# Experts stage: ScalarE puts the tokens into the PSUM bank and writes the bank out; one gate product moves to GpSimd

## The reference

```python
x = x + conv_ref(ln_c(x))        # instance norm, q/k/v, attention in 8x8 windows (4 heads of 8), projection
t = tokens(x)                    # per pixel 32 channels
t = t + ffn_ref(ln_t(t))         # the mixture of experts
# ffn_ref: router_probs = softmax(t @ router_w + router_b)  over 8 experts
#   top_p, top_i = top_k(router_probs, 2); top_p /= sum(top_p)
#   out = sum_k top_p[k] * (t @ expert_w[top_i[k]] + expert_b[top_i[k]])
```

## Time and profile before

| what | value |
|---|---|
| median of 3 runs | 396.82 us (395.78 to 398.11) |
| profiled execution, its own time | 396.52 us |
| its span | 394.4 us |
| TensorE / VectorE / ScalarE / GpSimd busy | 90% / 85% / 66% / 41% of the span |

### The profile page before, as it was taken

How to read it: one execution, slowest core, us unless ns; L and a number is a source line. 1 busy time by engine, 2 the same in 40 slices (tenths; PEclk the granted TensorE clock), 3 DMA queues, 4 the chain that set the end, 5 groups by cost and what they waited for, 6 DMA issues and landing times.

```text
span 394.4 us, 12569 instructions
## 1 busy us (share of the span) xinstructions
PE 355.4 (90%) x5318; PEld 186.3 (47%) x5318; DVE 334.9 (85%) x435; ACT 260.4 (66%) x448; POOL 162.4 (41%) x191
## 2 busy tenths in 40 slices
PE   5998599999999999999999999898889897768894
PEld 2556366566666656566566556465321221111121
DVE  1598989898898889998998889999878999996785
ACT  3665787878878888768788887764663674324431
POOL 8610000220220220786551220687783468348543
PEclk9999999999999999999999999999998999896998
DMA  7700000220000000000002000033223444443541
GB/s 308 299 3 3 2 3 2 55 57 2 4 2 3 2 2 3 2 2 3 2 3 57 3 2 2 3 78 79 62 66 102 136 128 111 131 125 94 148 141 53
DMA packets 12870, 22.49 MB, mean 57 GB/s; under 512 B 2960, under 2 KB 5136, under 8 KB 12432
## 3 DMA queue, kind: packets, MB, share of 16 engines
q1 hardware_dynamic: 12240, 19.93, 17.4%
q10 hardware_dynamic: 576, 1.77, 1.1%
HBM read 5.96 MB, written 4.19 MB: 26 GB/s over the span
## 4 chain that ended last, share of the span: by engine, by line
PE 62%; DVE 23%; ACT 6%; issue 6%; POOL 2%; DMA 1%; POOLq 0%; DVEq 0%; ACTq 0%
PE psum L611 13%; PE psum L628 9%; PE psum L596 7%; PE psum L636 4%; PE psum L547 4%; PE psum L762 4%; PE psum L571 3%; DVE neg_max L1156 3%; PE psum L444 3%; DVE probs L1299 3%; PE psum L566 3%; DVE window_work L1159 3%; PE psum L580 2%; PE psum L774 2%; DVE probs L1296 2%
## 5 line engine op out<-in xcount | busy, mean ns | idle before, releaser
L327 POOL TENSOR_TENSOR o_norm<-o_tok,o_rden 128x128 f32<-128x128 f32 x64 | 25.4, 417 | 169.6 <-DVE o_rden L1169 169.6
L611 PE MATMUL psum<-weights_sb,window_work 128*128 128x128 f32 x512 | 81.6, 281 | 6.4 <-DVE window_work L1159 4.2
L896 ACT ACTIVATE probs<-psum 128x512 f32<-128x512 f32 x128 | 74.7, 594 | 17.5 <-PE psum L611 15.3
L1159 DVE TENSOR_TENSOR window_work<-psum,neg_max 128x1024 f32<-128x1024 f32 x64 | 78.4, 1225 | 2.2
L611 PEld LDWEIGHTS psum<-weights_sb,window_work 128*128 128x128 f32 x512 | 57.2, 140 | 48.7 <-issue 27.8
L1156 DVE TENSOR_REDUCE neg_max<-psum 128x16 f32<-128x1024 f32 x64 | 76.8, 1199 | 1.5 <-PE psum L596 1.5
L628 PE MATMUL psum<-probs,v_cols 128*32 128x64 f32 x2048 | 54.8, 225 | 0.4 <-DVE o_tok L1167 0.2
L628 PEld LDWEIGHTS psum<-probs,v_cols 128*32 128x32 f32 x2048 | 34.8, 109 | 28.2 <-issue 24.8
L880 ACT ACTIVATE stage<-k_sb,weights_sb 128x512 f32<-128x512 f32 x64 | 44.1, 719 | 0.0
L1167 DVE STREAM_TRANSPOSE o_tok<-psum 128x512 f32<-128x512 f32 x32 | 22.9, 716 | 20.4 <-PE psum L628 20.3
L596 PE MATMUL psum<-stage 32*64 32x256 f32 x1024 | 35.8, 387 | 2.7 <-DVE window_work L1159 2.0
(11 more groups left out here) (131 smaller groups left out, 607.0 us busy)
## 6 DMA issues: line engine op xcount, KB each, us to landing
stage<-act_all SPq DMA_DIRECT2D x144, 64.0 KB, 2.0
out<-out_sb SPq DMA_DIRECT2D x16, 256.0 KB, 2.0
stage<-in_x SPq DMA_DIRECT2D x3, 1024.0 KB, 11.9
gate_rows<-gate_parts SPq DMA_DIRECT2D x16, 128.0 KB, 2.6
weights_sb<-weights ACTq DMA_DIRECT2D x1, 811.5 KB, 15.1
stage<-in_x SPq DMA_DIRECT2D x1, 768.0 KB, 5.0
gate_f<-gate_sel ACTq DMA_DIRECT2D x1, 512.0 KB, 11.1
weights_sb<-weights ACTq DMA_DIRECT2D x1, 320.0 KB, 7.9
```

Of the source, the lines that this page charges most:

```text
L327: last = pool.tensor_tensor(o_norm[:, hf, :, p * 16:p * 16 + 16].rearrange("p g (b d) -> p g b d", b=2), t[:, p * 8:p * 8 + 8, :].rearrang ...
L611: last = nc.tensor.transpose(bank[TURN_BANKS[v % 2]][:, b * P:b * P + P], heads.rearrange("p h k -> p (h k)"), const["c_ident"][:, :])
L896: nc.scalar.activation(probs[:, w % 4, :], bank[TURN_BANKS[w % 2]][:, :], ACT.Exp).then_inc(exp_done, 1)
L1159: nc.vector.tensor_tensor(shifted_unit[:, unit % 2, :, :, :], t, m_t.unsqueeze(3).to_broadcast([P, IMG, HEADS, TOK]), ALU.add).then_inc(sh ...
```

## The change

Chunks 2 to 15 no longer use `combine`. ScalarE's `preset_bank(c)` copies the tokens of chunk c from `act_all` into bank 6 or 7, `bias(c)` and the experts then add to them, and ScalarE's `write_out(c)` copies the bank to `out_sb`. Both stand in half 1 behind `copy_gates`: `write_out(c-1)`, then `preset_bank(c+1)`. VectorE keeps `combine(0)` and `combine(1)`. Step 21 of quads 2 and 3 moves from VectorE to GpSimd, and step 22 goes behind it, to the head of the next half. On SyncE the store of a chunk moves behind the `repeat_tokens` of the next iteration, and `move_gates(1)` moves from iteration 2 to iteration 1, ahead of `repeat_tokens(4)`.

```diff
--- before.py
+++ after.py
@@ -189,6 +189,7 @@
         gate_copied = sem("gate_copied")
         pool_scaled = sem("pool_scaled")
         y_step = sem("y_step")
+        preset = sem("preset")
         summed = sem("summed")
         stored = [sem(f"stored{u}") for u in range(2)]
 
@@ -198,6 +199,7 @@
         GATE_OPS = 30
         EARLY = 2
         REP_FIRST = 2
+        PRESET_FIRST = 2
 
         def slot(c):
 
@@ -246,7 +248,7 @@
 
         LATE_POOL = [[] for _ in range(2 * CHUNKS)]
         for quad in range(EARLY, QUADS):
-            for h, n in ((1, 6), (4, 14), (6, 22), (7, 23), (8, 26), (8, 27), (9, 29)):
+            for h, n in ((1, 6), (4, 14), (6, 21), (7, 22), (7, 23), (8, 26), (8, 27), (9, 29)):
                 LATE_POOL[late_half(quad, h)] += [(quad, n)]
 
         block = ctx.enter_context(nc.Block())
@@ -288,13 +290,20 @@
             move_gates(0)
             repeat_tokens(1)
             repeat_tokens(2)
+            def store(c):
+                sp.wait_ge(summed, c + 1)
+                sp.dma_start(out_v[:, c // BANDS, c % BANDS, :], out_sb[:, c % 2, :]).then_inc(stored[c % 2], 16)
+
             for c in range(CHUNKS):
+                if c == 1:
+                    move_gates(1)
                 if c + 3 < CHUNKS:
                     repeat_tokens(c + 3)
-                if c % QUAD == 2 and c // QUAD + 1 < QUADS:
+                if c % QUAD == 2 and 2 <= c // QUAD + 1 < QUADS:
                     move_gates(c // QUAD + 1)
-                sp.wait_ge(summed, c + 1)
-                sp.dma_start(out_v[:, c // BANDS, c % BANDS, :], out_sb[:, c % 2, :]).then_inc(stored[c % 2], 16)
+                if c >= 1:
+                    store(c - 1)
+            store(CHUNKS - 1)
             for u in range(2):
                 sp.wait_ge(stored[u], CHUNKS // 2 * 16)
 
@@ -418,7 +427,7 @@
                     h = 2 * c + eh
                     late = [(q, n) for q, n in LATE_POOL[h]]
                     for quad, n in late:
-                        if n == 23:
+                        if n in (22, 23):
                             gates(quad, n)
                     scale(c, eh)
                     if h == 0:
@@ -428,7 +437,7 @@
                     if h == 3:
                         early(CHUNKS + 1, 0)
                     for quad, n in late:
-                        if n != 23:
+                        if n not in (22, 23):
                             gates(quad, n)
 
 
@@ -766,14 +775,17 @@
 
             def bias(c):
 
-                wait_past(pe, summed, c - 1)
+                if c < PRESET_FIRST:
+                    wait_past(pe, summed, c - 1)
+                else:
+                    pe.wait_ge(preset, c + 1 - PRESET_FIRST)
                 if c == 1:
                     pe.wait_ge(x2_done, CHUNKS + X2)
                 quad = c // QUAD
                 pe.wait_ge(gate_step[quad], GATE_OPS + ONE)
                 nc.tensor.matmul(bank[6 + c % 2][:, :], const["c_eb"][:, c % QUAD, :],
                                  gate_f32[:, quad % 2 * CHUNK:(quad % 2 + 1) * CHUNK],
-                                 start=True, stop=False, skip_group_check=True)
+                                 start=(c < PRESET_FIRST), stop=False, skip_group_check=True)
 
             def side(c, eh):
 
@@ -1018,6 +1030,23 @@
                     nc.scalar.activation(x_rep[:, slot(c), b, :], bank[first_bank + b][:, :], ACT.Copy
                                          ).then_inc(rep_done, 1)
 
+            def write_out(c):
+
+                act.wait_ge(y_step, c * 2 + 2)
+                if c == PRESET_FIRST:
+                    act.wait_ge(summed, PRESET_FIRST)
+                act.wait_ge(stored[c % 2], c // 2 * 16)
+                nc.scalar.activation(out_sb[:, c % 2, :].rearrange("p (y win x) -> p win y x", win=NW, y=WS),
+                                     bank[6 + c % 2][:, :].rearrange("p (win y x) -> p win y x", win=NW, y=WS),
+                                     ACT.Copy).then_inc(summed, 1)
+
+            def preset_bank(c):
+
+                act.wait_ge(summed, c + 1 - PRESET_FIRST)
+                act.wait_ge(x2_done, c + 1 + X2)
+                nc.scalar.activation(bank[6 + c % 2][:, :], act_all[:, c * CHUNK:c * CHUNK + CHUNK], ACT.Copy
+                                     ).then_inc(preset, 1)
+
             exps(CHUNKS - 1, NW - 2)
             exps(CHUNKS - 1, NW - 1)
             late_act = {}
@@ -1028,6 +1057,11 @@
                 for eh in range(2):
                     quad, k = (c + 1) // QUAD + EARLY, (c + 1) % QUAD
                     copy_gates(c, eh)
+                    if eh == 1 and c >= 1:
+                        if c - 1 >= PRESET_FIRST:
+                            write_out(c - 1)
+                        if c + 1 < CHUNKS:
+                            preset_bank(c + 1)
                     if c * 2 + eh in late_act:
                         due, n = late_act[c * 2 + eh]
                         if n == 0:
@@ -1047,6 +1081,7 @@
                         elif k == 2:
                             token_deviations(quad)
                             keep_logits(quad, at=1)
+            write_out(CHUNKS - 1)
 
         @block.vector
         def _(dve):
@@ -1231,10 +1266,6 @@
                     one = v.tensor_tensor(small[:, p_best, :], small[:, near, :], small[:, rden, :], ALU.mult)
                 elif n == 20:
                     one = v.tensor_tensor(small[:, p_second, :], small[:, e_gap, :], small[:, p_best, :], ALU.mult)
-                elif n == 21:
-                    one = v.tensor_tensor(g(w.a), g(w.mask1), wide(p_best), ALU.mult)
-                elif n == 23:
-                    one = v.tensor_tensor(w.sum, w.a, w.b, ALU.add)
                 elif n == 24:
                     one = v.transpose(w.rest, w.sum)
                 one.then_inc(gate_step[quad], 1)
@@ -1279,7 +1310,7 @@
 
             divide(CHUNKS - 1, 1)
 
-            HALF_STEPS = ((0, 1, 2), (3, 4, 5), (7, 8), (9, 10, 11, 12), (13,), (15, 16), (17, 18, 19, 20, 21), (24,))
+            HALF_STEPS = ((0, 1, 2), (3, 4, 5), (7, 8), (9, 10, 11, 12), (13,), (15, 16), (17, 18, 19, 20), (24,))
 
             def steps(c, eh):
 
@@ -1304,12 +1335,11 @@
                     if (c, eh) == (0, 1):
                         dve.wait_ge(x2_done, CHUNKS - 1 + X2)
                         residual(CHUNKS - 1, bank_at=TURN_BANKS[1])
-                    if eh == 0 and c >= 1:
+                    if eh == 0 and 1 <= c <= PRESET_FIRST:
                         combine(c - 1)
                     if (c, eh) == (0, 1):
                         early(CHUNKS, 1)
                     steps(c, eh)
-            combine(CHUNKS - 1)
 
 
 # ---- launch: one core; the host lays the weights out in blocks per image ----
```

## The result

The changed kernel takes 393.0 us (median of 4, 392.7 to 393.1) against 397.12 us (median of 4, 395.78 to 398.11) for the kernel before on the same chip: ratio 0.9897, 95% interval 0.9866 to 0.9928. It is 4.1 us faster. The forecast was 392.1 us, 4.7 faster, with a range of 389.6 to 394.9. A second measurement on another occasion gave 393.0 us and 0.990 (0.9871 to 0.9929).

The account below looks back on a forecast made before the run. VectorE was taken to bound chunks 3 to 9 (97% busy), a TensorE-VectorE loop the late chunks. Gains of 4.3 us at chunk 10, 0.1 at the end and 0.3 for lengthened products total 4.7: 392.1 us, range 389.6 to 394.9.

Parts of the forecast that it names:

- Step 21: Chunks 5 and 9: about 0.6 us off VectorE's queue each; GpSimd's longer chain brings `scale` 0.5 later.
- The combines: Fourteen leave VectorE: seven in its full stretch worth 4.2 us at most, five in the late loop 0, the last 0.1.
- Chunks 3 to 6: Chunk 5's L1296 2.0 us earlier, limited by TensorE, where VectorE alone gives 2.4; chunk 6 stands 2.1 early.
- Chunks 7 to 9: Three more combines at 0.60 us, VectorE-bound, none lost: 1.8 more, so chunk 9's step 20 ends at 349.2.
- the one for the shared lock: VectorE products with two SBUF inputs lengthen beside GpSimd's; 0.3 us added for L1224's chance 0.9 in chunk 8.
- Chunk 10: Its L1296 at 356.6 with TensorE at 2.4 GHz or 359.0 at 1.2 GHz; the middle, 357.8, taken: gain 4.3 us.
- T: The end of VectorE's step 20, at 353.14 us in chunk 9 before the change and forecast at 349.2 after.
- The end: The last combine, at 391.25 us, is on the path; ScalarE takes its place with 0.60 for 0.69: 0.1 gained.
- the stretch at 296.90 to 300.30 stays: A low-clock stretch of TensorE ahead of all that changes, forecast to remain.
- the sign that the prediction named as wrong: TensorE at 1.2 GHz in a stretch between 300 and 340 us, one of several observations that would count against the forecast.

Follow-up runs that it names:

- The late five: Changed kernel with ScalarE's preset and write-out for chunks 11 to 15 only and step 21 on VectorE; 395.25 us, ratio 0.9976 to the kernel before.
- the middle eight: Changed kernel with ScalarE's preset and write-out for chunks 2 to 9 only and step 21 on VectorE; 392.64 us, ratio 0.990 to the kernel before.

## Why the prediction was right

**The combines: right, and in the right place.** The late five are worth little (0.9976) and the middle eight carry the gain (0.990), as the full stretch of VectorE said and the busy shares of the span did not. The spacing of the late loop was 5.49 before and after, and SyncE's order alone brought nothing.

**Chunks 3 to 6: right to 0.1 in one execution, in part by luck.** Chunk 5's product was forecast 2.0 earlier and came 1.97 earlier (322.34 less 320.37); it has TensorE's gate product in front of it, 0.38 idle. Chunk 6's was forecast 2.1 earlier: 329.91 less 1.64 is 328.27, where the trace before has 330.35, 2.08. But 0.26 of it is a stretch at 1.2 GHz in chunk 2 that was absent, and in the second execution, where it was present, the two products came 1.6 and 1.7 earlier. So the limit that TensorE sets in chunk 5 was there, and the agreement to 0.1 is luck.

**Chunks 7 to 9: right in kind, too small in the first execution.** Step 20 of chunk 9 was forecast 3.9 us earlier and came 5.8 earlier. The term that was mis-sized is the one for the shared lock, put at 0.3. L1244 took 0.69 in chunk 3 (at 307.80) and in chunk 7, 1.31 and 1.32 before, and L1259 0.69 in chunk 8 where it took 1.62. In chunk 3 a later step lengthened by 0.95 and took that back; in chunks 7 and 8 the 0.6 and the 0.9 stayed. The rest, 0.3, is again chunk 8, which before had a stretch at 1.2 GHz (from 341.2 to 344.6, a third one that the prediction did not read). GpSimd now waits instead. Its `scale` products, 1.27 to 1.28 as a rule, took 1.75 to 1.79 four times between 300 and 347. In the second execution the 0.9 did not go (L1259 took 1.66) and step 20 of chunk 9 came 3.4 earlier, less than forecast: the prediction's remark that such a 0.9 appears or goes by chance of the shift held.

**Chunk 10: the term was taken from the middle, and it was the low end.** Forecast T + 7.4 at 2.4 GHz and T + 9.8 at 1.2 GHz; measured 358.71 less 349.02, T + 9.7, at a clock of 0.51. `scale` ended at T + 5.0 (forecast T + 4.9) and step 24 waited 1.95 (forecast 1.9). Too much time forecast at chunk 9 and too little at chunk 10 nearly cancelled: 5.1 us earlier from the stage's start, forecast 4.3. In the second execution chunk 10's product came 3.2 earlier. The forecast lies between the two, so its closeness to the median is in part luck as well.

**The end: right, too small to see.** ScalarE's last write-out began 1.12 us behind the start of the last experts products, as VectorE's combine had, and took 0.60 for 0.69.

**Step 21: nearly right in the change, wrong alone.** I charged the longer chain 0.5 and booked the 0.6 on VectorE. Alone it costs 2.5 us, through idle time of TensorE and the clock behind it. In the full change the runs with and without it don't differ beyond noise (0.990 and 0.9915), and one trace of each shows it bringing 0.8 by chunk 9 and costing 1.6 from there to chunk 10. That the move pays in the full change is not shown.

**The clock.** The prediction said that the stretch at 296.90 to 300.30 stays, since it lies ahead of all that changes. It wasn't there in the first execution of the kernel after, and was in the second. The second also has the sign that the prediction named as wrong, 1.2 GHz between 300 and 340 us: a stretch from 338.2 to 341.6. It stands in chunk 8, where the kernel before has one too, so it is no new fall. Which stretches fall is not fixed by the code alone, so a single profiled execution of this kernel can't carry a claim of less than about 2 us. The Trainium skill ("TensorE: Matmul & The Clock Gate", section "HAM oscillation — how this bites in real kernels") tells of a kernel whose waits between bursts of matmuls bring the low clock back in each iteration. The traces agree so far as the falls shown here stand behind a wait of TensorE, as that of 1.98 us in the run with presets doubled. But a wait alone is not enough: for the logits in chunk 2 TensorE waited 1.50 us in the trace before (up to 295.14) and fell, and 1.49 in the first execution after (up to 296.77) and did not. What decides between two executions of the same code was not tried.

**Left open.** How much of the measured 4.1 us is VectorE's time and how much is fewer low stretches can't be told from one trace for each kernel. Low stretches of 13.6 us stood in the stage in the trace before, and 7.0 and 13.6 in the two of the kernel after, each without the last one at the very end; both measurements of the kernel after have the same median of 393.0. The granted clocks of all executions give a bound. Their mean is 0.979 over the seventeen of the kernel before that ran beside the second measurement, and 0.986 over the ten of the kernel after. Taken as shares of two levels, that is 16.6 and 10.9 us at 1.2 GHz. Products take about twice as long in such a stretch (1.93 for 1.07), so it costs at most half its length, and my estimate is that at most 2.9 of the 4.1 us can be the clock. It is probably less: among the seventeen a higher clock did not go with a shorter time.

## What to carry to other kernels

Read which engine is full in the stretch where the work stands, and count only the removed instructions that stand there: eight of fourteen carried as much gain as all. Before moving work to an engine with idle time, look for the place where that engine's queue stands ahead of TensorE, since 1.15 us of GpSimd in each of two chunks cost 2.5 us, and 0.6 of ScalarE in one chunk 2.1, once TensorE's clock fell behind the wait. Where waits end nearly together, as those for the square root and for GpSimd's chain did, taking away one shows little. And profile the same kernel twice before an agreement to 0.1 us is believed: here two executions differed by 2.3.

## What the runs showed of the hardware

- VectorE instructions with two SBUF inputs lengthened from 0.69 to 1.31 and 1.62 when they began under a GpSimd product that had 0.77 and 1.07 us left, so by most of that rest, and GpSimd products lengthened from 1.27 to 1.75 when they began just behind such a VectorE one; `combine`, with one input in PSUM, took 0.68 to 0.69 throughout. VectorE's busy time fell by 12.4 us where the removed instructions account for 10.9; the 1.5 between them are such lengthenings that fell away (0.6, 0.6, 0.9, 0.3 and 0.2, less a new one of 0.95).
- ScalarE writes a PSUM bank of 128x512 float32 from SBUF in 0.60 us, the same as it reads one.
- Filler products on TensorE did not pay. One moved a fall of the clock from chunk 10 to chunk 11, ten short ones did not keep the products behind them from 1.2 GHz (0.9933 against 0.990).
- The same program's two profiled executions differed by 2.3 us at chunk 9 of the experts stage, by which stretches ran at 1.2 GHz and by one lengthened instruction.
